# VectorE's order in each step: the addition of x moved from behind the next tile's low part to directly behind the gate product

## The reference, cut to what matters

```python
x = x + ga * _L0_attn_ref(h, ...)
h = _layernorm(x, axis=-1) * (1 + cb) + sb
x = x + gb * _L0_ffn_ref(h, L0_ffn_weight, L0_ffn_bias)
# _L0_ffn_ref: blocks of 32 numbers of h are divided by max|h|/7.5, rounded to the
# grid of a 6-bit float, scaled back, and multiplied by the weight (quantised too); bias is added
```

## Time and profile before

| what | value |
|---|---|
| runs of the kernel | 359.78 us median of 3 (359.64 to 360.4) |
| the profiled execution, its own time | 357.79 us |
| its span, first to last instruction | 355.9 us |
| mean granted TensorE clock | 0.963 of full |
| VectorE busy | 287.7 us in 515 instructions |
| ScalarE busy | 239.4 us |
| VectorE's idle time ahead of low parts (L1162) | 44.2 us |
| ScalarE's idle time ahead of presets (L456) | 33.9 us |

### The profile page before, as it was taken

The page is one execution under the profiler, slowest core; times in us unless marked ns, Lnnn a source line. Parts: engine busy times, 40 slices in busy tenths (PEclk is TensorE's granted clock), DMA queues, the critical chain, the costliest instruction groups (busy, mean ns, idle before and its releaser), DMA issues. The chain is left out here.

```text
span 355.9 us, 6057 instructions
## 1 busy us (share of the span) xinstructions
PE 308.5 (87%) x2157; PEld 229.0 (64%) x2157; DVE 287.7 (81%) x515; ACT 239.4 (67%) x536; POOL 226.6 (64%) x121
## 2 busy tenths in 40 slices
PE   7979997575999799979989999689989978993992
PEld 5215556465888576767777777477867766682881
DVE  4677959939769997969788979797879989899743
ACT  3387815596976788878788898957869896221320
POOL 1367395084965697859897887876959695904000
PEclk9999999789999899999999999989999999998798
DMA  7999999966289767977796768666966991111024
GB/s 208 395 407 397 341 305 260 253 231 88 32 185 251 108 234 118 290 152 253 116 315 122 257 121 309 123 252 109 262 151 169 227 210 46 75 68 50 17 106 145
DMA packets 23971, 69.00 MB, mean 194 GB/s; under 512 B 2387, under 2 KB 2516, under 8 KB 19974
## 3 DMA queue, kind: packets, MB, share of 16 engines
q1 hardware_dynamic: 16400, 53.93, 44.0%
q0 software_dynamic: 7392, 14.68, 25.0%
q10 hardware_dynamic: 150, 0.02, 0.0%
HBM read 51.48 MB, written 17.14 MB: 193 GB/s over the span
## 5 line engine op out<-in xcount | busy, mean ns | idle before, releaser
L717 PE MATMUL ps<-WH,XH 128*128 128x512 f32 x256 | 109.8, 431 | 10.0 <-ACT XH L447 9.9
L717 PE MATMUL ps<-WL,XH 128*128 128x512 f32 x256 | 103.7, 407 | 0.0
L377 POOL TENSOR_TENSOR U<-U,c_bc 128x1024 f32<-128x1024 f32 x31 | 75.3, 2429 | 37.6 <-ACT U L467 36.9
L1162 DVE TENSOR_TENSOR XL<-ps,XH 128x512 fp32r<-128x512 f32 x64 | 43.9, 687 | 44.2 <-ACT XH L447 43.9
L388 POOL TENSOR_TENSOR U<-U,sb_bc 128x1024 f32<-128x1024 f32 x31 | 74.2, 2394 | 2.5
L717 PE MATMUL ps<-WH,XL 128*128 128x512 f32 x256 | 69.4, 393 | 3.1 <-DVE XL L1162 3.1
L467 ACT ACTIVATE U<-X,nmr,rstd 128x512 f32<-128x512 f32 x64 | 48.3, 806 | 35.1 <-DVE nmr L1174 30.8
L717 PEld LDWEIGHTS ps<-WH,XH 128*128 128x128 f32 x256 | 50.6, 198 | 22.9 <-ACT ps L456 11.2
L456 ACT COPY ps<-bias_bc 128x512 f32<-128x512 f32 x61 | 35.4, 581 | 33.9 <-DVE X L1227 33.7
L717 PEld LDWEIGHTS ps<-WH,XL 128*128 128x128 f32 x256 | 48.4, 190 | 14.8 <-DVE XL L1162 3.9
L717 PEld LDWEIGHTS ps<-WL,XH 128*128 128x128 f32 x256 | 50.8, 198 | 9.3
(11 more groups left out here) (211 smaller groups left out, 345.5 us busy)
## 6 DMA issues: line engine op xcount, KB each, us to landing
X<-in_x SPq DMA_DIRECT2D x16, 1024.0 KB, 5.9
out<-X SPq DMA_DIRECT2D x15, 1024.0 KB, 6.5
X<-mod_scratch POOLq DMA_DIRECT2D x14, 1024.0 KB, 10.0
X<-in_wmod SPq DMA_DIRECT2D x2, 1024.0 KB, 12.1
sb_bc<-mod_scratch SPq DMA_DIRECT2D x7, 256.0 KB, 8.8
c_bc<-mod_scratch SPq DMA_DIRECT2D x7, 256.0 KB, 8.7
gb_bc<-mod_scratch SPq DMA_DIRECT2D x7, 256.0 KB, 6.3
msp<-mod_scratch SPq DMA_DIRECT2D x8, 160.0 KB, 9.8
```

The source lines that it names most:

```text
L377: nc.gpsimd.tensor_tensor(a, a, spread(c_bc[:, b % 2, :]), ALU.mult).then_inc(u_done, 2 if g == 0 else 1)
L717: return M(bank, a[:, n % 2, k * P:(k + 1) * P], w[:, k, :], start=False, stop=last, skip_group_check=n >= 3)
L1162: TT(XL[:, n % 2, :], ps[:, XT_BANK + n % 2, :], XH[:, n % 2, :].bitcast(F32), ALU.subtract).then_inc(xl_done, 1)
```

## The change

In steps 2 to 62 VectorE's addition of tile q-1 stands directly behind the gate product of that tile, and the low part of tile q+1 behind both. In steps 0 and 1, and for the last tile, nothing changes. No other engine's list changes, and no wait or instruction is added or removed.

```diff
             for q in range(LAST):
                 if q >= 2:
                     times_gate(q - 1)
+                if q >= 2:
+                    add_tile(q - 1)
                 if 1 <= q < LAST - 1:
                     low_part(q + 1)
-                if q >= 2:
-                    add_tile(q - 1)
                 for g, h in halves(q, NORMAL, 9):
                     if h == 0:
                         scales(g)
```

## The result

The changed kernel took 357.24 us, median of 20 runs (355.81 to 360.62); the kernel before took 360.98 in 20 runs beside them (358.63 to 363.55). The ratio is 0.9918, interval 0.9891 to 0.9946: about 3.0 us faster. Forecast was 4.75 us off. Direction and range (352.0 to 359.0) hold; the size came out at six tenths, and 357.24 lies just above the 353 to 357 that was given as likeliest. A ratio leaves out runs over 1.5% above the fastest of their kernel, none of them here, but two of the six with the stands alone in experiment 2, where the means of all runs are 4.8 us apart and the medians 3.9, against 5.9 by the ratio.

The account below looks back on a forecast made before the run. The prediction took VectorE and ScalarE, setting each other's pace, as the bound, with TensorE following. Gains of 7.20 less losses of 2.99 plus 0.54 at the end took 4.75 us off 359.78, giving 355.0 us, range 352.0 to 359.0.

Parts of the forecast that it names:

- The two prices: Per step on VectorE: 0.60 us gained where the low part has to wait, 0.13 us lost where it does not.
- (b): In steps without a wait, the addition directly behind the gate product it reads costs 0.13 us more; 2.99 us in all.
- Rival 1: VectorE's addition starts 0.60 us behind its gate product, so the losses vanish: 7.74 us off, 352.0 us; chance 0.12.
- (a): Where VectorE waits ahead of a low part, the addition runs inside that wait, gaining 0.60 us.
- The end: Behind the last tile's low part, the last gate product goes at 346.8 instead of 347.34, so the span ends 0.54 us earlier.
- The ring: ScalarE's stretch from scales to a high part, then VectorE's from that low part to the next scales; 16.06 us becomes 15.7.
- The stall thus goes from ScalarE's preset to its normalisation: ScalarE waits less for additions at presets, from 33.7 us clearly down, and as long or longer for scales; no gain.
- 12 low parts gain 0.60 each: Twelve VectorE low parts with waits on the path, from near 77 us to 310.69, gain 7.20 us together.
- GpSimd's work starts from ScalarE's normalisations and moves with them: GpSimd's work was taken to come earlier along with ScalarE's, and was costed at nothing.
- Rival 2: TensorE, 87% busy, uses up its idle stretches in most groups; half the gains go, 2.4 us off, 357.4; chance 0.16.
- rival 4: Slower: each further TensorE stretch at 1.2 GHz costs 1.30 us, five give 361.5; chance 0.11 with anything else slower.

Follow-up runs that it names:

- the stands alone: New order only in 24 steps where VectorE waited ahead of the low part, old order elsewhere; against the kernel before 0.9836 (355.82 us), later 0.9853 (355.56 us).
- experiment 2: Two kernels against the kernel before: new order only in 24 steps where the low part waited, 0.9836; only in all the others, 1.0077.
- the light TensorE: Four of twelve matmuls of each product left out from the fourth tile on; against the kernel before, old order 0.9898 (356.94 us), new order 0.9792 (352.38 us).
- the repeat: The changed kernel run again without edits, for a second profile; 357.19 us, 0.9928 of the kernel before.
- short stores: Stores of whole groups write only one eighth of their columns; in the new order 357.50 us, 0.9933 of the kernel before.
- experiment 4: Whole-group stores cut to one eighth of their columns, in both orders, against the kernel before: old order 360.32 us (0.9998), new order 357.50 us (0.9933).

## Why the prediction was right in kind and too large

**The two prices hold.** (b): 0.70 to 0.74 between gate product and addition in all 64 tiles; the losses measured as one term came to 2.8 us (1.0077) for the 2.99 forecast. Rival 1, the free neighbour, is out; so is the rule from the Trainium skill that the prediction weighed ("VectorE: DVE Perf Modes", section The DRAIN you can't avoid), as far as it would make this semaphore free. (a): where nothing else interferes a stand gives 0.59 to 0.62, as in the sections up to 99.77, 242.30 and 260.98 of the column for stands alone, and in the one up to 349.51 without the twelve products' difference.

**The end holds.** 0.54 forecast, 0.49 to 0.60 in every profile with the new order at the end and TensorE's full work. With the light TensorE it is 0.00: 7.24 us from the last gate product to the end in either order.

**The ring holds.** 15.74 us for the 15.7 forecast, with ScalarE's wait at its presets down from 33.7 to 26.8. But "The stall thus goes from ScalarE's preset to its normalisation" failed: at the normalisations it stayed, 30.9 for 30.8, and it grew at the wait for the transposes, 18.3 for 10.3. TensorE had less to spare than the prediction gave it.

**The term that was mis-sized is the gain, "12 low parts gain 0.60 each", 7.20 us.** With the end it makes 7.74; the stands alone measured 5.9 and 5.3, the first of them 4.8 by the means of all its runs. The prediction took each of the twelve to reach the next scales whole, cut only by the losses of 0.13. In its place the runs showed:
- The first of the twelve, near 77 us, gave nothing: its 0.60 was eaten by the copy that GpSimd holds. VectorE has no stand between that low part and the next scales, so the 0.59 that the copy lasted longer is the whole account. The prediction called VectorE continuous there and took its durations for fixed; the 0.96 of that copy was in the trace, twice the 0.47 of its twin.
- The one near 192 us: with two or three losses 0.21 to 0.34 was due in the section up to 203.87, and 0.60 with the stands alone; -0.40 and -0.91 came (in one profile -3.50, with a stand of 3.91 of ScalarE's sums for the added x; in the repeat of the stands alone -1.77, with one of 1.69). "GpSimd's work starts from ScalarE's normalisations and moves with them" was the sentence that failed: it also starts from loads of x, and these did not come earlier with the ring (the issue that waits for this one ran 138.94 us behind the first gate product in the repeat, for 136.20 before). With short stores the section gained 0.21. That a load's lateness reaches the ring through GpSimd is shown by the rows of experiment 4; that full stores are what makes it late is likely but has the rival named there, and what it costs on average over executions is open.
- Up to 116.46 us TensorE holds high parts back, because the ring comes earlier and, in some executions, because TensorE stays at its lower clock for longer behind 92 us. Rival 2 (TensorE takes over) and rival 4 (its clock) are each true in this one stretch and nowhere near the five of its kind that rival 4 needed. (Rival 4's 1.30 for the products at 330.34 is the price of a stretch that was at the lower clock only in its first part: the clock of the last 2.1 us was 0.82.) The size differs by execution, 0 to 1.1 us, in the old order as well, and stays open.
- In the other sections of the changed kernel the losses behind a stand are two or three, as forecast: 0.33 is 0.60 - 2 x 0.13, 0.19 to 0.21 is 0.60 - 3 x 0.13.
- With the stands alone there are no such losses, and still only a few sections gain 0.60; the one up to 277.04 gains 0.21. There the new stand of experiment 2 takes most of the rest. In the changed kernel the losses fall into that wait, so leaving them out saves less than 0.13 each.
- Against these stands a gain that wasn't counted, and so luck: 0.37 to 0.81 in the section up to 99.77.

The section table doesn't add up column by column. In the section up to 349.51, with +0.83 and +0.33 in the parts and -0.19 in the whole, that is the twelve products (without them 0.62, -0.48 and 0.09); in the one up to 277.04, with +0.21 and -0.28 against +0.32, it is the new stand. And the sums of the profile columns aren't the timed results, because the profiled executions lie anywhere in a scatter of about 1% to each side.

## What to carry to other kernels

Price an in-order engine's instructions by what they depend on: a neighbour that reads the last result cost 0.13 us more than an independent one, so a reordering pays in the steps where the engine stands and costs in others; apply it step by step, which here gave up to twice the gain. A gain of one engine ends where the next one isn't ready: look how long the others in the ring have worked without a pause before counting it whole. When a chain is moved ahead, list every input of every engine that follows it: those that come from DMA, or from an engine that doesn't move, need not come earlier with it, and can take the gain back. And an instruction that lasts twice as long as its twin may be waiting inside, as here; find out for whom before counting on what is ahead of it.

## What the runs showed of the hardware

A VectorE instruction can be held by GpSimd without any semaphore, and the trace shows it as a longer duration: a 1x512 copy in SBUF took 0.40 to 0.47 us alone and 0.96 or 1.55 beside a GpSimd TENSOR_TENSOR, ending 0.27 to 0.28 us behind it in each case; a maximum with both operands in SBUF took 0.68 alone and 1.83 beside it. VectorE's instructions with an operand in PSUM, as L1162 and L1227, kept their 0.68 to 0.69 beside the same kind of GpSimd work. This agrees with the Trainium skill, "SBUF — State Buffer", section Who interferes with whom, by which copies in a two-port mode, and instructions with two SBUF inputs beside a GpSimd instruction that reads SBUF, share a port pair with GpSimd, held for a whole instruction. In which mode this copy ran, no run here shows.
